# Attention over 64 latents in a four-stage layer kernel: one value matmul of 128 columns for latents and remainders, and denominators summed by the exponentials

## What is computed

```python
ckv_l = rms_norm(ckv[..., :KVLR], kv_a_ln_w)          # 64 latents per position
kv = (ckv_l @ w_kvb.T).reshape(b, s, H, DN + DV).transpose(0, 2, 1, 3)
k_nope, v = (kv[..., :DN], kv[..., DN:])
scores = jnp.einsum('bhqd,bhkd->bhqk', q_full, k_full) * scale
scores = jnp.where(causal, -jnp.inf, scores)
attn = jax.nn.softmax(scores.astype(jnp.float32), axis=-1).astype(q_full.dtype)
out = jnp.einsum('bhqk,bhkd->bhqd', attn, v)
```

## Time and profile before

| | before |
|---|---|
| median of 3 runs | 1887.69 us (1885.84 to 1889.42) |
| the profiled execution, its own time | 1888.36 us |
| its span, first to last instruction | 1886.3 us |
| TensorE: matmuls busy / weight loads busy | 1624.6 / 1323.9 us |
| VectorE busy | 1261.5 us |
| ScalarE busy | 984.7 us |
| GpSimd busy | 332.3 us |
| instructions | 38115 |

### The profile page before, as it was taken

How to read it: one execution, slowest core, us unless ns; L and a number is a source line. 1 busy time by engine, 2 the same in 40 slices (tenths; PEclk the granted TensorE clock), 3 DMA queues, 4 the chain that set the end, 5 groups by cost and what they waited for, 6 DMA issues and landing times. The chain is left out here.

```text
span 1886.3 us, 38115 instructions
## 1 busy us (share of the span) xinstructions
PE 1624.6 (86%) x14452; PEld 1323.9 (70%) x14452; DVE 1261.5 (67%) x2637; ACT 984.7 (52%) x1929; POOL 332.3 (18%) x765
## 2 busy tenths in 40 slices
PE   3679998999999999999999999999489999772697
PEld 1457777777777777777777877877468778651486
DVE  3846676776776777777777777777455454478445
ACT  2436665665665666666666666666343222272432
POOL 3411111121111212111211211110100000073311
PEclk9879999999999999999999999999789999975699
DMA  7000000000000000000000000000121000010000
GB/s 221 1 1 2 2 2 1 2 2 2 2 2 2 2 2 1 1 2 2 2 2 2 2 2 1 2 2 2 37 64 30 1 1 1 1 54 0 1 12 34
DMA packets 23252, 23.52 MB, mean 12 GB/s; under 512 B 9356, under 2 KB 20492, under 8 KB 22948
## 3 DMA queue, kind: packets, MB, share of 16 engines
q1 hardware_dynamic: 17764, 14.77, 2.7%
q10 hardware_dynamic: 5312, 6.33, 1.2%
HBM read 19.00 MB, written 2.10 MB: 11 GB/s over the span
## 5 line engine op out<-in xcount | busy, mean ns | idle before, releaser
L711 ACT ACTIVATE pT_hi<-pT 128x512 f16<-128x512 f32 (+3 forms) x640 | 340.6, 532 | 367.5 <-PE pT L629 364.3
L832 DVE TENSOR_TENSOR pT_lo<-pT,pT_hi 128x512 f16<-128x512 f32 (+3 forms) x640 | 388.1, 607 | 158.9 <-ACT pT_hi L711 153.7
L820 DVE TENSOR_REDUCE cmx<-pS 128x1 f32<-128x512 f32 x576 | 347.8, 617 | 98.1 <-PE pS L616 94.3
L700 ACT ACTIVATE pr<-pS,nmx 128x512 f32<-128x512 f32 (+3 forms) x640 | 398.4, 623 | 11.1 <-DVE nmx L823 10.0
L629 PE MATMUL pT<-ident,pr 128*128 128x128 f32 x2176 | 346.2, 275 | 9.8 <-DVE pT_lo L832 6.3
L611 PE MATMUL pS<-lT_hi,qT_hi 128*128 128x512 f32 (+2 forms) x640 | 284.7, 445 | 57.8 <-ACT pr L700 48.4
L629 PEld LDWEIGHTS pT<-ident,pr 128*128 128x128 f32 x2176 | 258.2, 140 | 43.8 <-ACT pr L700 10.1
L671 PE MATMUL pO<-c_hi,pT_hi 128*128 128x65 f16 x2176 | 265.8, 194 | 1.2 <-DVE O L850 0.6
L672 PE MATMUL pO<-c_lo,pT_hi 128*128 128x65 f16 x2176 | 266.6, 193 | 0.0
L673 PE MATMUL pO<-c_hi,pT_lo 128*128 128x65 f16 x2176 | 263.7, 192 | 0.0
L616 PE MATMUL pS<-lT_hi,qT_lo 128*128 128x512 f32 (+2 forms) x640 | 257.3, 402 | 0.0
(11 more groups left out here) (270 smaller groups left out, 2914.8 us busy)
## 6 DMA issues: line engine op xcount, KB each, us to landing
X<-in_x SPq DMA_DIRECT2D x4, 512.0 KB, 6.9
wo<-in_w_o ACTq DMA_DIRECT2D x1, 2048.0 KB, 14.3
out<-X SPq DMA_DIRECT2D x4, 512.0 KB, 2.6
raw<-in_wd SPq DMA_DIRECT2D x14, 128.0 KB, 2.1
raw<-in_wg SPq DMA_DIRECT2D x13, 128.0 KB, 2.7
raw<-in_wu SPq DMA_DIRECT2D x13, 128.0 KB, 2.7
wqn<-in_w_qn ACTq DMA_DIRECT2D x1, 1536.0 KB, 17.9
intg<-in_qg SPq DMA_DIRECT2D x1, 768.0 KB, 5.5
```

The lines of the kernel that those rows point to most:

```text
L700: act.activation(pr[:, at % RING, 0:n * P], pS[at % 4][:, 0:n * P], ACT.Exp, bias=nmx[:, p % 4:p % 4 + 1]).then_inc(sem("exped"), 1)
L711: act.activation(pT_hi[:, a % 4, 0:chunk[a][2] * P], src, ACT.Copy).then_inc(sem("t_hi"), 1)
L820: ch.inc(dve.tensor_reduce(cmx[:, p % 2, c:c + 1], pS[at % 4][:, 0:n * P], AX.X, ALU.max))
L832: dve.tensor_tensor(pT_lo[:, a % 4, 0:w], src, pT_hi[:, a % 4, 0:w], ALU.subtract).then_inc(sem("t_lo"), 1)
```

## The change

The latents and their remainders move side by side into one array `c_both` of 128 columns per tile, without the columns of ones and zeros. Per block, `values` makes one matmul of hi with all 128 columns and one of lo with the first 64, where there were three of 65; a row's quarter of pO is now 128 columns wide, and the whole bank is in use. Each exponential also gives the sum of its chunk (`accum_out`) into `part`, 16 rows x 4 chunks; a wait protects the reuse of `part`. `o_out` adds the chunk sums, copies the second halves (hi x c_lo) out of pO, takes the reciprocals, adds the first halves to the copy, and multiplies. Three memsets go.

```diff
-            c_hi = sbr(heads_in, "c_hi", [P, NT, 66], F16)
-            c_lo = sbr(heads_in, "c_lo", [P, NT, 66], F16)
+            c_both = sbr(heads_in, "c_both", [P, NT, 2 * KVL], F16)
+            c_hi, c_lo = c_both[:, :, 0:KVL], c_both[:, :, KVL:2 * KVL]
...
-                        pool.memset(c_hi[:, :, 64:65], 1.0)
-                        pool.memset(c_hi[:, :, 65:66], 0.0)
-                        ch.inc(pool.memset(c_lo[:, :, 64:66], 0.0))
...
-                rl = sbr(loop, "rl", [P, 2, HG])
+                part = sbr(loop, "part", [P, 16, 4])
+                rl = sbr(loop, "rl", [P, 2, 2, HG])
+                both = sbr(loop, "both", [P, 2, HG, KVL])
...
-                            o = pO[:, p % HG * (KVL + 1):(p % HG + 1) * (KVL + 1)]
+                            o = pO[:, p % HG * 2 * KVL:(p % HG + 1) * 2 * KVL]
...
-                                pe.matmul(o, hi, c_hi[:, j, 0:KVL + 1], start=(j == 0), stop=False)
-                                pe.matmul(o, hi, c_lo[:, j, 0:KVL + 1], start=False, stop=False)
-                                m = pe.matmul(o, lo, c_hi[:, j, 0:KVL + 1], start=False, stop=(j == tile_at(p)))
+                                pe.matmul(o, hi, c_both[:, j], start=(j == 0), stop=(j == tile_at(p)))
+                                m = pe.matmul(o[:, 0:KVL], lo, c_hi[:, j], start=False, stop=(j == tile_at(p)), skip_group_check=True)
...
                             if c == 0:
                                 act.wait_ge(sem("maximum"), p + 1)
+                                if p % HG == 0 and p >= 4 * HG:
+                                    act.wait_ge(sem("o_out"), p // HG - 3)
...
                             act.activation(pr[:, at % RING, 0:n * P], pS[at % 4][:, 0:n * P], ACT.Exp,
-                                           bias=nmx[:, p % 4:p % 4 + 1]).then_inc(sem("exped"), 1)
+                                           bias=nmx[:, p % 4:p % 4 + 1], accum_out=part[:, p % 16, c:c + 1]).then_inc(sem("exped"), 1)
...
-                            o = pO[:, 0:HG * (KVL + 1)].rearrange("p (h d) -> p h d", h=HG)
-                            r = rl[:, i % 2, :]
-                            ch.inc(dve.reciprocal(r, o[:, :, KVL]))
+                            o = pO[:].rearrange("p (h d) -> p h d", h=HG)
+                            total, r, s_ = rl[:, i % 2, 0, :], rl[:, i % 2, 1, :], both[:, i % 2]
+                            n_c = tiles_in_order[u] // 4 + 1
+                            ch.inc(dve.tensor_reduce(total, part[:, HG * i % 16:HG * i % 16 + HG, 0:n_c], AX.X, ALU.add))
+                            ch.inc(dve.tensor_copy(s_, o[:, :, KVL:2 * KVL]))
+                            ch.wait()
+                            dve.reciprocal(r, total).then_inc(sem("dve_step"), 1)
+                            dve.tensor_tensor(s_, o[:, :, 0:KVL], s_, ALU.add).then_inc(sem("dve_step"), 1)
+                            ch.n += 2
                             ch.wait()
                             dve.tensor_tensor(O[:, u % OR, g * HG * KVL:(g + 1) * HG * KVL].rearrange("p (h d) -> p h d", h=HG),
-                                              o[:, :, 0:KVL], r.unsqueeze(2).to_broadcast([P, HG, KVL]), ALU.mult).then_inc(sem("o_out"), 1)
+                                              s_, r.unsqueeze(2).to_broadcast([P, HG, KVL]), ALU.mult).then_inc(sem("o_out"), 1)
```

## The result

The changed kernel takes 1937.03 us (median of 4 runs, 1934.64 to 1939.29) where the kernel before takes 1887.06 (4 runs, the three of the table above among them): 1.0263 times as long, 95% interval 1.0245 to 1.0281. That is 50 us more; 52 were forecast. The profiled execution took 1936.18 us, span 1934.4.

The account below looks back on a forecast made before the run. The loop was taken to be bound by a ring through TensorE and ScalarE, not TensorE's work. From 1888.4 us, -3 + 24 + 31 = +52 gave 1940 us; range 1908 to 1968, about 8 in 10.

Parts of the forecast that it names:

- The bound: Attention loop: held by a ring through TensorE and ScalarE, not by TensorE's work, though TensorE is busy 93 to 95%.
- the stops: TensorE's weight load before score matmuls: 146 waits for an exponential and 93 for "issue", 124 us in all.
- the ring: Attention loop: transposes end, ScalarE copies them out, then runs the exponential, for whose PSUM bank TensorE's next scores wait.
- Part 1: Value matmuls on TensorE: 88 ns per block for 90, counting on 670 of 2176 blocks, -3 us.
- Rival (c): Value matmuls: the wide matmul doesn't hide its weight load, up to +34 us for -3, 1977 at most; chance 0.09.
- Part 2: Exponentials that sum on ScalarE: each read instruction costs 0.10 us, counted at 239 waits before scores, +24 us.
- Rival (b): Summing exponentials on ScalarE: reads cost their full 0.20 us, 48 us for 24, 1964; chance 0.08.
- Part 3: End of a group on VectorE: +0.90 us at each of 64, less slack, 25 and 6 us by halves, +31 together.
- Rival (a): Ends of groups: VectorE's delay is absorbed in pauses and only the reads remain, 1909 us; chance 0.12.
- tens of waits: Second half of the loop: TensorE's single 0.6 us wait for a group's result becomes tens of entries.
- Rival (d): Whole loop: TensorE's stream decides everywhere, reads and additions go into idle time, 1879 to 1884 us; chance 0.05.

Follow-up runs that it names:

- The exchange of order: Kernel before with ScalarE taking the exponential of a row's last chunk directly behind the one before it, ahead of the next copy out of pT: 1860.51 us, ratio 0.9854.
- the small activation: Kernel before with a one-column activation, result unused, after each exponential, whose own signal isn't delayed: 1891.10 us, ratio 1.0012.
- the longer ends alone: Kernel before with only VectorE's longer end of a group (small reduction, copy, reciprocal, element-wise maximum, multiplication from SBUF): 1919.34 us, ratio 1.0164.
- the pair exchanged: Changed kernel with a row's last exponential directly behind the one before it on ScalarE, ahead of the next copy: 1927.88 us, ratio to before 1.0217.

## Why the prediction was right, and where it wasn't

**The bound** was read rightly, and this carried the rest: busy shares would have named TensorE, whose stream gives at most 9 us by the forecast's own prices; the stops named the ring. The exchange of order shows it, 27 us for no work saved.

**Part 1, -3 us:** -2.5, with 85 ns per block where I had 88 and, from the bare clock, 86. That only a part of the blocks lies on the path holds: 5 ns on all 2176 would be 11 us, and the interval ends at 5. That the part is just a third (3.4 us) fits, but the interval, 1.7 to 5.1 us, is too wide to show it. Rival (c), the wide matmul with an exposed load, is out, and with it the rule of the Trainium skill, "TensorE: Matmul & The Clock Gate", section "Back-to-back issue gap", of about 81 ns in a sustained stream: the trace shows 50 to 60 ns with a load before every matmul, in a stream that alternates 128 and 64 columns. Its isolated figure of about 56 is the one that fits.

**Part 2, +24 us:** 21 alone (23.2 within the loop), 24 when taken out of the changed kernel. The price per stop, 0.10 us, came from one row of another stage, and the row of 13 blocks grew by just two of them. That it counts at the stops, as later signal and not as queue time, is borne out by the small activation, 3 us for 21. The count was a little coarse: it spread the reads by the stops, 10 and 14 us for the halves, where 7 and 16 were measured. Rival (b), the full 0.20, is out.

**Part 3, +31 us:** 31 alone, 24.4 and 6.9 by halves for 25 and 6. The length was 0.85 us for 0.90, in part since the addition out of PSUM took 0.39 for 0.42. Following each of the 64 places to its first pause was worth the work: the full price would have been 54. VectorE's chain and the maxima in the first half, the group's result in the second, are also the two ways that the waits show. Rival (a), absorbed, is out.

**A sign that came weaker than I wrote it:** I expected tens of waits of the first value matmul for the group's result in the second half. In the changed kernel there were 9 in all, of 4.8 us, 7 of them and 4.4 us in that half; with the longer ends alone 13 and 7.3 us, which is about the 6.9 us lost there. My own working had only 11 such places, so "tens" was never in it. The larger part goes by the maxima: in the changed kernel the exponentials wait 27.4 us for them where it was 10.0, and the transposes 16.5 us for remainders where it was 6.3.

**Rival (d)**, TensorE's stream decides, would have hidden both delays; neither was.

**Where luck had a hand:** the sums' price was 3 us too high for the first half of the loop and 2 us too low for the second, and in the total these cancel. And every price holds for the order of before only: with the pair exchanged the same change costs 67 us.

## What to carry to other kernels

A matmul saved counts by its columns and by whether anyone stands for it: three of 65 columns and one of 128 with one of 64 are the same stream, 90 and 85 ns, and here most of even that lay under stops (2.5 of 11 us came through). Work moved from a busy engine to an idle one isn't free when its result is on the way that the busy engine waits for: look for the ring, count how often it is closed, and price the move by its delay and not by the idle share. And look first at the order inside the ring: exchanging one pair of instructions in each longer row was worth 27 us, more than the value matmuls of this change could have brought if all of their 11 us had counted, and once it is made the prices of the other parts are new ones.

## What the hardware showed that I had not expected

The sum of an activation costs a second instruction of 0.20 us, but only 0.09 to 0.10 us of the queue, and the same of delay to the signal, at 512 columns with a bias as at 64 without; a one-column activation costs the queue the same. A copy of 128x256 four-byte elements out of PSUM on VectorE took 0.414 us (the groups view of the changed kernel: 26.5 us for 64), about as long as an element-wise operation of two tensors of that size (0.39 out of PSUM and SBUF, 0.43 from SBUF, in the same view).
